# A mask in idle rows of the exponent products, end factors in 64x64 tiles, and two moved steps, in a state-space and feed-forward kernel

## What is computed

```
x = x + layernorm(attn(layernorm(x)))          # attn: a state-space scan
x = x + layernorm(ffn(layernorm(x)))
attn:  xi = u Wx^T, z = u Wz^T; x = silu(causal_conv4(xi));  b = x Wb^T, c = x Wc^T (8 heads x 64)
       dt = softplus(x Wdt^T + b_dt);  a = -exp(log_a)
       state = exp(dt a) state + (dt b) x^T;   y = c . state   (per head 64x64, step by step)
       y = y + d x; normalised per head over all tokens; * silu(z); Wout^T
ffn:   gelu(x sign(w1)^T alpha1 + b1) sign(w2)^T alpha2 + b2
```

## Time and profile before

| | us |
|---|---|
| three runs | 1372.21, 1370.19, 1371.21 |
| median | 1371.21 |
| the profiled execution | 1372.45 |
| its span, first to last instruction | 1370.7 |

### The profile page before, as it was taken

The page is one execution under the profiler, slowest core; times in us unless marked ns, Lnnn a source line. Parts: engine busy times, 40 slices in busy tenths (PEclk is TensorE's granted clock), DMA queues, the critical chain, the costliest instruction groups (busy, mean ns, idle before and its releaser), DMA issues.

```text
span 1370.7 us, 27653 instructions
## 1 busy us (share of the span) xinstructions
PE 1286.9 (94%) x10552; PEld 812.6 (59%) x10552; DVE 1008.7 (74%) x2364; ACT 746.8 (54%) x1270; POOL 491.5 (36%) x551
## 2 busy tenths in 40 slices
PE   6998999999999999999999999999999999999675
PEld 3564647565575756656575655757556565666543
DVE  5565786869777696877868688686968768685575
ACT  5564664647655485554745567454855547455321
POOL 2030435134441543224442344414443254332533
PEclk9899999999999999999999999999999999999888
DMA  7010000101010010101001010000101000010100
GB/s 220 1 48 16 2 0 2 47 1 48 0 48 1 3 46 1 48 1 47 1 1 47 2 47 1 23 26 1 47 1 48 1 30 3 1 33 1 32 1 31
DMA packets 30563, 32.88 MB, mean 24 GB/s; under 512 B 1856, under 2 KB 28628, under 8 KB 30432
## 3 DMA queue, kind: packets, MB, share of 16 engines
q1 hardware_dynamic: 30432, 31.11, 7.2%
HBM read 22.72 MB, written 8.39 MB: 23 GB/s over the span
## 4 chain that ended last, share of the span: by engine, by line
PE 40%; DVE 25%; issue 16%; POOL 13%; ACT 6%; POOLq 0%; DVEq 0%; ACTq 0%
PE bank L1383 22%; PE bank L1558 5%; POOL Cd L774 4%; DVE xs L1046 4%; PE bank L1543 4%; POOL y L739 3%; DVE hh L1241 2%; DVE un L1021 2%; POOL xdw L769 2%; PE bank L1525 2%; POOL state L785 2%; DVE gn_stats L1165 1%; DVE sh L1051 1%; ACT L950 1%; DVE uh L1230 1%
## 5 line engine op out<-in xcount | busy, mean ns | idle before, releaser
L1383 PE MATMUL bank<-sh,WbT 128*128 128x512 f16 x768 | 177.2, 387 | 10.6 <-DVE sh L1051 10.6
L1383 PE MATMUL bank<-sh,WcT 128*128 128x512 f16 x768 | 175.9, 379 | 0.0
L960 ACT ACTIVATE mt<-bank 128x512 f32<-128x512 f32 x128 | 69.5, 597 | 186.7 <-PE bank L1465 186.7
L1046 DVE SCALAR_TENSOR_TENSOR xs<-xi,vectors,xs 128x512 f32<-128x512 f32 x192 | 152.5, 804 | 7.5 <-ACT xs L876 3.2
L769 POOL TENSOR_TENSOR xdw<-xdt,decays 128x512 f32<-128x512 f32 x64 | 66.7, 1042 | 236.8 <-DVE xdt L1133 236.8
L1383 PEld LDWEIGHTS bank<-sh,WbT 128*128 128x128 f16 x768 | 74.2, 99 | 101.8 <-issue 15.3
L1558 PE MATMUL bank<-uh,sign1T 128*128 128x512 f16 x512 | 122.8, 386 | 7.5 <-DVE uh L1230 7.2
L1543 PE MATMUL bank<-WoutT,yT 128*128 128x256 f32 x512 | 117.4, 386 | 12.6 <-POOL yT L753 6.5
L1383 PEld LDWEIGHTS bank<-sh,WcT 128*128 128x128 f16 x768 | 75.2, 98 | 86.5
L988 ACT ACTIVATE hf<-bank,vectors,alpha 128x512 f32<-128x512 f32 x128 | 99.5, 777 | 45.8 <-PE bank L1558 33.6
L1571 PE MATMUL bank<-sign2T,hh 128*128 128x256 f16 x1024 | 119.3, 275 | 1.8 <-DVE hh L1241 1.8
(11 more groups left out here) (186 smaller groups left out, 2539.5 us busy)
## 6 DMA issues: line engine op xcount, KB each, us to landing
xt<-L_attn_input_tensor_dram SPq DMA_DIRECT2D x16, 512.0 KB, 5.0
u<-L_attn_input_tensor_dram SPq DMA_DIRECT2D x16, 512.0 KB, 4.0
out_dram<-u SPq DMA_DIRECT2D x16, 512.0 KB, 2.9
yT<-in_L_ffn_w_dram SPq DMA_DIRECT2D x2, 512.0 KB, 9.6
u<-in_L_ffn_w_dram SPq DMA_DIRECT2D x2, 512.0 KB, 8.9
BT<-in_L_attn_Wx_dram SPq DMA_DIRECT2D x1, 512.0 KB, 4.7
BT<-in_L_attn_Wz_dram SPq DMA_DIRECT2D x1, 512.0 KB, 5.6
zs<-in_L_attn_Wb_dram SPq DMA_DIRECT2D x1, 512.0 KB, 5.5
```

The costliest lines, as they stand in the source:

```text
L960: nc.scalar.activation(mt[n % 2][:, g].rearrange("p c t -> p (c t)"), bank(t, ("seg", j, q, g))[:, :], ACT.Exp).then_inc(seg_exp.sem, 1)
L1046: nc.vector.scalar_tensor_tensor(out=xs[:, c, :], in0=xi[:, c, k:k + BLK], scalar=taps[:, c, k:k + 1], in1=xs[:, c, :], op0=ALU.mult, op1= ...
L1383: mm = nc.tensor.matmul(bank(t, key)[:, :], w[i][:, k, cols(m)], v[h][:, k, :], start=(a == 0), stop=(a == len(terms) - 1))
```

## The change

1. The mask product is left out. cum now has a half of the rows for each half g of the heads: 64 rows with, of four copies, two as targets and two as sources. For half g, `of_source[g]` and `of_target[g]` have cum in the 64 rows of g, and in the other 64 rows an identity of 64 against the mask, so that one product of 128 rows gives difference and mask. The identity reaches 64 targets, so each seg bank takes two products, each of 4 x 64 columns, that differ in the mask rows.
2. E is a step of its own, "ends". It is made by two products, each with 64 rows and 64 output partitions, 512 columns wide, to the two halves of one bank. It comes ahead of "front" for chunk 0 and right behind "carry" of chunk q-1 for chunk q, on TensorE, ScalarE (exponent) and GpSimd (times C) alike.
3. VectorE's work on cum is split. "cums" keeps the high and low split; a new step "roles" behind "uT" writes cum_target and cum_source, then of_target and of_source for both halves (six operations for two). "decay" writes da and two halves of da_wide, three operations for one.
4. "in_stat" of the next block moves from between the parts of C to behind "front" of chunk 0, "in_norm" to behind "carry" and "ends" in chunk 1's place.
5. The setup has two more masks and other selection vectors.

```diff
-        steps += own(("C", j, 0), ("cums", j)) + tail(("uT", j)) + own(("skip", j), ("C", j, 1)) + tail(("H", j, 0), ("H", j, 1))
+        steps += own(("C", j, 0), ("cums", j)) + tail(("uT", j)) + own(("roles", j), ("skip", j), ("C", j, 1)) + tail(("H", j, 0), ("H", j, 1))
-        steps += [(who, "in_stat", nj)] + own(("C", j, 2)) + tail(("H", j, 2), ("H", j, 3)) + [(who, "in_norm", nj)]
+        steps += own(("C", j, 2)) + tail(("H", j, 2), ("H", j, 3))
...
-        steps += own(("decays", j), ("front", j, 0)) + tail(("O", j, 0))
+        steps += own(("decays", j), ("ends", j, 0), ("front", j, 0)) + [(who, "in_stat", nj)] + tail(("O", j, 0))
...
-        steps += own(("carry", j, 0)) + tail(("O", j, 1)) + own(("back", j, 0), ("front", j, 2), ("score", j, 2))
-        steps += own(("carry", j, 1), ("back", j, 1)) + tail(("end_stat", j)) + own(("front", j, 3), ("score", j, 3))
-        steps += [(who, "xT", nj, 0)] + own(("carry", j, 2), ("back", j, 2)) + [(who, "xT", nj, 1)]
+        steps += own(("carry", j, 0), ("ends", j, 1)) + [(who, "in_norm", nj)] + tail(("O", j, 1)) + own(("back", j, 0), ("front", j, 2), ("score", j, 2))
+        steps += own(("carry", j, 1), ("ends", j, 2), ("back", j, 1)) + tail(("end_stat", j)) + own(("front", j, 3), ("score", j, 3))
+        steps += [(who, "xT", nj, 0)] + own(("carry", j, 2), ("ends", j, 3), ("back", j, 2)) + [(who, "xT", nj, 1)]
...
-        of_source = sb("of_source", [P, NQ, HP, P], F16)
-        of_target = sb("of_target", [P, KI, P], F16)
+        cum_target = sb("cum_target", [P, P], F16)
+        cum_source = sb("cum_source", [P, P], F16)
+        past = [cum, cum_target, cum_source]
+        of_source = [sb(f"of_source{g}", [P, NQ, 2, P], F16) for g in range(HP)]
+        of_target = [sb(f"of_target{g}", [P, KI, P], F16) for g in range(HP)]
...
-                nc.vector.tensor_scalar(da_wide[:, :, :], da_raw[:, :, :].rearrange("p q h -> p (q h)")[:, None, :]
-                                        .to_broadcast([P, PARTS, NQ * HEADS]), DECAY_FLOOR, None, ALU.max)\
-                    .then_inc(dt_step.sem, 1)
+                raw = da_raw[:, :, :].rearrange("p q h -> p (q h)")
+                nc.vector.tensor_scalar(da[:, :], raw, DECAY_FLOOR, None, ALU.max).then_inc(dt_step.sem, 1)
+                for g in range(HP):
+                    v = of_side(raw, g)[:, None].to_broadcast([P, PARTS, NQ * KI // 2, 2])
+                    nc.vector.tensor_scalar(da_wide[:, g, :, :].rearrange("p m (n f) -> p m n f", f=2), v, DECAY_FLOOR, None,
+                                            ALU.max).then_inc(dt_step.sem, 1)
...
+            def roles(t, j):
...
+                nc.vector.tensor_scalar(cum_target[:, :], cum[:, :], target[:, 0:1], minus_source[:, 0:1], ALU.mult, ALU.add)\
+                    .then_inc(cum_roles.sem, 1)
+                nc.vector.tensor_scalar(cum_source[:, :], cum[:, :], source[:, 0:1], target[:, 0:1], ALU.mult, ALU.add)\
+                    .then_inc(cum_roles.sem, 1)
+                for need in latest(full(s, ("seg", sj, NQ - 1, HP - 1)), full(s, ("E", sj, NQ - 1))):
+                    dve.wait_ge(*need)
...
+                for g in range(HP):
+                    rows = rows_of(g)
+                    nc.vector.tensor_tensor(of_target[g][rows, :, :], cum_target[rows, None, :].to_broadcast([HALF, KI, P]),
+                                            pair_mask[rows, :, :], ALU.mult).then_inc(ends_made.sem, 1)
+                for g in range(HP):
+                    rows = rows_of(g)
+                    nc.vector.tensor_tensor(of_source[g][rows, :, :, :],
+                                            cum_source[rows, None, None, :].to_broadcast([HALF, NQ, 2, P]),
+                                            chunk_mask[rows, :, None, :].to_broadcast([HALF, NQ, 2, P]), ALU.mult)\
+                        .then_inc(ends_made.sem, 1)
...
-                    nc.tensor.matmul(bank(t, key)[:, :], ident_h[:, :], past[:, None, :].to_broadcast([P, KI, P]),
-                                     start=True, stop=False)
-                    nc.tensor.matmul(bank(t, key)[:, :], of_source[:, q, g, :],
-                                     of_target[:, :, :].rearrange("p c t -> p (c t)"), start=False, stop=True)\
-                        .then_inc(full_sem(t, key), 1)
+                    for a in range(2):
+                        part = slice(a * HALF, (a + 1) * HALF)
+                        mm = nc.tensor.matmul(bank(t, key)[:, :].rearrange("p (c t) -> p c t", c=KI)[:, :, part],
+                                              of_source[g][:, q, a, :], of_target[g][:, :, part], start=True, stop=True)
+                    mm.then_inc(full_sem(t, key), 1)
...
+            def ends(t, j, q):
+
                 key = ("E", j, q)
+                if q == 0:
+                    pe.wait_ge(*ends_made.count(t, j * 2 * HP + HP))
                 pe.wait_ge(*empty(t, key))
-                nc.tensor.matmul(bank(t, key)[:, :], of_source[0:HALF, q].rearrange("p g s -> p (g s)")[:, HALF:HALF + P],
-                                 of_target[0:HALF, :, :].rearrange("p c t -> p (c t)"), start=True, stop=True)\
-                    .then_inc(full_sem(t, key), 1)
+                for g in range(HP):
+                    rows = rows_of(g)
+                    mm = nc.tensor.matmul(bank(t, key)[rows, :], end_mask[rows, q, :],
+                                          of_target[g][rows, :, :].rearrange("p c t -> p (c t)"), start=True, stop=True)
+                mm.then_inc(full_sem(t, key), 1)
```

More of the change, by code:

```diff
@@ L384, in uses @@
             if kind == "front":
-                return [*[("seg", *at, g) for g in range(HP)], ("X", *at), ("Bt", *at), ("E", *at)]
+                return [*[("seg", *at, g) for g in range(HP)], ("X", *at), ("Bt", *at)]
+            if kind == "ends":
+                return [("E", *at)]
             if kind == "score":
@@ L474, in mamba_sandwich_kernel @@
         C_out = Signal(sem("C_out"), NJ * KI)
-        DT = 8
+        DT = 8 + HP
         dt_step = Signal(sem("dt_step"), NJ * DT)
@@ L711, in _ @@
                                pattern=[[-1, P]], channel_multiplier=1).then_inc(masks_made, 1)
-            pool.affine_select(out=past[:, :], in_=past[:, :], compare_op=ALU.is_ge, fill=PAST, base=0,
-                               pattern=[[1, P]], channel_multiplier=-1).then_inc(masks_made, 1)
+            for n, base in enumerate((0, HALF, -HALF)):
+                pool.affine_select(out=past[n][:, :], in_=past[n][:, :], compare_op=ALU.is_ge, fill=PAST, base=base,
+                                   pattern=[[-1, P]], channel_multiplier=1).then_inc(masks_made, 1)
             pool.wait_ge(masks_made, MASKS_MADE)
@@ L807, in _ @@
                 "O": add_bias, "end_add": add_middle,
-                "gate": gate, "front": front, "carry": carry}
+                "gate": gate, "front": front, "ends": ends, "carry": carry}
             all_batches(pool, handlers)
@@ L993, in _ @@
                 "z_in": gate_in, "z_silu": gate_silu, "silu": x_silu, "xs": x_high, "dt": step_exp,
-                "log": step_log, "cums": cum_top, "skip": skip_term, "C": project_c, "decays": decay_exp, "front": front,
+                "log": step_log, "cums": cum_top, "skip": skip_term, "C": project_c, "decays": decay_exp, "front": front, "ends": ends,
                 "gate": head_normalise, "uT": middle_high, "H": hidden})
@@ L1307, in _ @@
                 "conv": convolve, "xs": x_low,
-                "dt": step_in, "log": step_mid, "decay": step_out, "B": project_b, "cums": decay_ends, "front": front, "score": score,
+                "dt": step_in, "log": step_mid, "decay": step_out, "B": project_b, "cums": decay_split, "roles": roles, "front": front, "score": score,
                 "carry": carry, "back": back, "head_stat": head_stats, "gn_sum": head_moments, "gn_root": head_variance,
@@ L1441, in running_sums @@
                 pe.wait_ge(*empty(t, key))
-                nc.tensor.matmul(bank(t, key)[:, 0:P], da_wide[:, :, :].rearrange("p a n -> p (a n)"), upto[:, :],
+                nc.tensor.matmul(bank(t, key)[:, 0:P], da_wide[:, :, :, :].rearrange("p g a n -> p (g a n)"), upto[:, :],
                                  start=True, stop=True).then_inc(full_sem(t, key), 1)
@@ L1448, in decay_sums @@
                 pe.wait_ge(*empty(t, key))
-                nc.tensor.matmul(bank(t, key)[:, 0:NQ * HEADS], after[:, :], da, start=True, stop=True)
+                nc.tensor.matmul(bank(t, key)[:, 0:NQ * HEADS], after[:, :], da[:, :], start=True, stop=True)
                 for g in range(HP):
                     mm = nc.tensor.matmul(bank(t, key)[g * HD:(g + 1) * HD, NQ * HEADS:NQ * (HEADS + KI)], ones[:, 0:HD],
-                                          of_side(da, g), start=True, stop=True)
+                                          of_side(da[:, :], g), start=True, stop=True)
                 mm.then_inc(full_sem(t, key), 1)
@@ L1576, in _ @@
```

(2 more changed lines are left out.)

96 lines of the change are left out of this document (53 added, 43 removed).

## The result

The changed kernel takes 1347.58 us, the median of 4 runs from 1343.99 to 1348.03; the kernel before, run beside it, 1370.70. The ratio is 0.9822, 95% interval 0.9809 to 0.9836. The profiled execution took 1347.90 us with a span of 1346.2; the spans differ by 24.5 us, at a mean granted clock of 0.982 in both.

A forecast was written before the change was run, and what follows sets the result against it. TensorE, busy 94%, was taken to bound the kernel by its start-to-start pitch. Terms 26.9 - 5.3 + 2.2 + 3.0 - 3.2 - 0.6 = 23.0 us gave 1348 us (1348.2 against the median), range 1338 to 1362.

The forecast's parts named there:

- A: Exponent products in each chunk: four of 256 columns at 0.112 each replace four of 512, saving 26.9 us.
- B: End factors' pair behind the carry: side by side at 0.22, 0.11 more in chunks 1 to 3, 5.3 us lost.
- C: Middle of the block: seven H waits for uh go, some 4.6 us; three-operation "decay" loses 2.4; net +2.2 us.
- D: GpSimd's order at block ends and batch starts: state's addition, yT additions and xh come sooner, +3 us, bounds 0 and 7.
- E: Input norm moved: nothing in batches 1 to 7, batch 0 loses; -3.2 us, bounds 0 and 6.8.
- F: Kernel start: extra memsets, selects and small operations ahead of the first statistics, 0.6 us lost, bounds 0 and 0.9.
- Rival 4: Exponent products: pieces of 64 columns stream at half rate, pitch 0.217, so A saves nothing: 1375 us; chance 0.04.
- Rival 1: End factors: a chunk's two products run one behind the other, writing one bank; 13.8 us more, 1362; chance 0.10.
- Rival 2: Chunk stage: freed TensorE time becomes waits on VectorE, its normalisations stretched beside GpSimd; 10 us in 14 blocks, 1358; chance 0.17.
- batch 0 about as long as before: Sign to look for: the first batch keeps about its old length, since E's loss is about all it gains.
- Rival 3: More than forecast: end factors mostly under the carry's tail, or VectorE's block ends gain a full microsecond; 1341 us; chance 0.12.

The follow-up runs named there:

- doubled products: Changed kernel with each pair issued twice: end factors' pairs 1358.25 us; in a separate run, exponent products' pairs 1371.57 us.
- experiments 7 and 8: 7: changed kernel, "roles" ahead of uT, 1390.87 us. 8 (late place alone): kernel before, only of_target and of_source moved behind uT, 1363.86 us.
- Experiment 5: Changed kernel with the end factors' pair moved from behind the carry to behind the transposes of its own quarter, on all engines: 1351.89 us.

## Why the prediction was right

1348.0 was forecast and 1347.58 measured. The span fell by 24.5 us against a sum of 23.0; the terms, for the whole kernel:

| term | forecast | measured | from |
|---|---|---|---|
| A exponent products | +26.9 | +26.9 | 0.87 to 0.45, 64 chunks |
| B end factors | -5.3 | -4.3 | 0.20 less 0.11, 48 chunks |
| C middle | +2.2 | +6.2 | 7 x (1.02 less 0.14) |
| D GpSimd's order | +3.0 | about +2.1 | 1.2 below, and what is left of 24.5 |
| E and F, batch 0 and start | -3.8 | -4.7 | 4.6 in the chunk stages, 0.1 at the start |
| waits for mt in batch 0 | none | -0.9 | also with the norm back |
| clock in batch 0 | none | -0.8 | +1.5 ahead of the first C, -2.3 behind 104 us |

**A** is the step that carries the change, and it was right to the last digit: 256 columns in four pieces of 64 have the pitch of the FFN's plain 256. Rival 4 is out, by the timeline and by the doubled products.

**B** was right. The pair costs 0.20 us in its place and 0.22 by itself. Rival 1 is out. The Trainium skill, "TensorEngine Tiling (Array Packing)", Restrictions and Gotchas, says that different row tiles cannot access one bank at the same time; by that the two would have taken turns. The Trainium skill, "PSUM — Partial Sum Buffer", section "PSUM bank collisions raise a hardware error", tells column tiles, which may share a bank, from row tiles, which may not. A diagonal pair differs in both. The measurement decides: 0.22 for both. In chunk 0 the pair's new place changed nothing: 0.09 us more ahead of it, 0.10 less behind the transposes.

**C** failed twice, both times in size. The gain at H was taken as the printed wait for uh, 4.6 us, and is 7.1 by the pitch (7 x 1.02); the run with the late place alone shows it. The loss at un was worked out from the printed 0.23 of da_wide, three operations for one, and TensorE shows 0.14 in place of 0.35: its first wait for un is 0.40 instead of 0.26, the next 0.40 in both. Small operations overlap as products do. VectorE's timeline before has da_wide at 667.87 and the next operation at 668.01; after:

```profile
659.65 0.18 DVE L1115 TENSOR_SCALAR da<-da_raw 128x32 f32<-128x32 f32 x1
659.75 0.29 DVE L1118 TENSOR_SCALAR da_wide<-da_raw 128x64 f32<-128x64 f32 x2
659.95 1.40 DVE L1029 BATCH_NORM_STATS2 stats_ff<-u 128x6 f32<-128x256 f32 x4
```

One takes 0.14 from start to start and three take 0.30: 0.16 more, which is the wait's 0.14. "roles" took 3.0 us for 2.6 and cost nothing, as forecast. H's waits went for the reason given, shown from both sides by experiments 7 and 8.

**D** named the wrong places. State's factor no longer waits behind Cd, but TensorE's two waits that should have used it are as they were: 0.71 from the last xdw to its carry and 0.61 at xi, before and after. What did go is TensorE's wait of 0.4 for xdt, which the kernel before has in three batches (554.40, 877.35 and 1278.35 us, 1.2 us or a little more), and 0.05 a block that no single row explains. Experiment 5 shows that the pair's place is worth 4.2 us in all, but by the pitch beside the carry and by xdt, not by state.

**E** was right for batches 1 to 7, to 0.01 us a batch, and too small for batch 0. The step that failed is "its 1.38 less some 0.3 of slack, 1.1 us for each block": xn takes 2.39 and 2.14 us there, because of the Cd product that term D had just put beside it, and TensorE waits 1.60 and 1.92. In the chunk stages in_norm costs 3.9 us for 2.2 and in_stat 0.7 for 1.0. Rival 2 had this stretch and placed it in the later batches, where the cover holds. Two more parts no term had. Without the move, too, the chunk stages of batch 0 gain only 1.9 of the 2.8 us that A and B measure there: TensorE waits 0.4 us for mt at the first end factors and 0.4 longer for ScalarE's mt in the second block. And the clock: behind the two waits for sh that either kernel has (1.36 and 1.94 us, up to 107.07), B, dt and B up to the first C took 14.87 us in the profiled execution of the changed kernel (to 121.94), and 12.58 before (107.53 to 120.11). But the kernel before had its longer low stretch ahead of its first C (clock 0.92 from 42 to 66 us) and lost 1.45 us there, so the clock cost 0.8 in all. The sign "batch 0 about as long as before" failed: it was 3.6 us longer.

**F**, 0.6 for the start, was 0.06: the first statistics start at 6.04 us, before at 5.99, with 0.43 of the idle time left. So the masks cost VectorE's slack and nothing else.

Rival 3 is out: the pair hides no more than forecast, and the block ends gave less. The hit within 0.4 us is partly luck: C gave 4 us more than forecast and B 1, and D and batch 0 took 3.5 back. The clock has a part in it as well: in the changed kernel's eight runs 0.982 is the usual mean and 0.985 comes twice, while the kernel before has 0.985 in 24 of the 37 runs beside the experiments. What stays open is what decides where in batch 0 the clock falls. From 99 to 115 us it was 0.68 to 0.75 in five of the seven profiled executions that have the whole move, and 0.89 in the two with doubled products, which have it too; it was 0.89 in all five that lack it or have only half.

## What to carry to other kernels

Take both gains and costs from start to start: the printed waits missed a third of the gain at H, and the printed length of small operations doubled the loss at un. Before moving an operation into an engine's gap, look which other engine's operation the same change puts beside it, and check the first round by itself, where the work that covers the gap in the steady state is missing. A part that brings nothing in seven batches of eight and costs in the first is best left where it was: without the norm's move the kernel is at 1343.10 us.

## What the runs showed of the hardware

- One f32 normalisation of 128x256 on VectorE takes 0.40 us alone (printed), and beside GpSimd's product of 1.26 us one of the four took 1.16 us in a later batch and 1.42 in batch 0; the four took 1.38 without it and 2.13 to 2.39 with it. The Trainium skill, "SBUF — State Buffer", section "SBUF: two separate sides", has a GpSimd instruction and a VectorE instruction that runs in a two-port mode, or has two SBUF inputs, take a shared pair of ports in turns, each for its whole length. If the normalisation is such an instruction, which no run here shows, the loss would be at most the 1.26 us of the product; 0.75 and 1.0 us are measured, which fits.
- Two products on diagonal 64x64 tiles, 512 columns each, into one bank: 0.22 us for both (0.53 less 0.31 behind the carry).
- TensorE at half its clock behind waits: eight products of 512 columns took 3.25 us behind a wait of 2.77, against 1.89 for the next eight; and 36 took 9.70 us from start to start in place of 7.76 in batch 0 of the changed kernel, where the stretch's granted clock was 0.72 of the 2.4 GHz level. Runs of one kernel lie up to 5.7 us apart (0.4 for the one with the norm back), mostly in the order of their mean clock; that is more than most terms above.
